# Tanh layer of a four-layer graph network on one Trainium2 core: the gate multiplies the vector weights first, the products go unreduced into the one-hot matmul in four column quadrants, and are folded once per group

## The reference, cut to what matters

```python
xs = concatenate([x[src, :8], x[dst, :8]])                 # 16 scalars per edge
xv = concatenate([x[src, 8:].reshape(E, 8, 3), x[dst, 8:].reshape(E, 8, 3)])
y1, y2 = _sph(edge_vec)
h = 2.0 ** 0.5 * relu(emb @ W1 / 10.0 ** 0.5)              # 16 hidden numbers per edge
w = (h @ W2 / 16.0 ** 0.5).reshape(E, 7, 16, 8)
wa_s, wb_s, wa_g, wb_g, wc, wd, we = [w[:, i] for i in range(7)]
s_out = PW_S * (einsum('eu,euw->ew', xs, wa_s) + INV_SQRT3 * einsum('eui,ei,euw->ew', xv, y1, wb_s))
g_out = PW_S * (einsum('eu,euw->ew', xs, wa_g) + INV_SQRT3 * einsum('eui,ei,euw->ew', xv, y1, wb_g))
v_out = PW_V * (INV_SQRT3 * einsum('eu,ek,euw->ewk', xs, y1, wc) + INV_SQRT3 * einsum('eui,euw->ewi', xv, wd)
                + einsum('eui,ea,iak,euw->ewk', xv, y2, W3J121, we))
s_act, gates = TANH_GAIN * tanh(s_out), TANH_GAIN * tanh(g_out)
edge_ftr = concatenate([s_act, (gates[:, :, None] * v_out).reshape(E, 24)]) * norm[:, None]
return segment_sum(edge_ftr, edge_dst, num_segments=N)
```

## Time and profile before

| | us |
|---|---|
| median of 3 runs (15111.97 to 15116.88) | 15116.87 |
| span of the profiled execution | 15106.0 |
| what lies around the span, against the median | 10.87 |
| stage of `window_pass_1` (first to last `prod`) | 4497.2 to 9752.3 |
| busy over the whole span: VectorE / TensorE matmuls | 12521.1 / 11855.8 |

### The profile page before, as it was taken

How to read it: one execution, slowest core, us unless ns; L and a number is a source line. 1 busy time by engine, 2 the same in 40 slices (tenths; PEclk the granted TensorE clock), 3 DMA queues, 4 the chain that set the end, 5 groups by cost and what they waited for, 6 DMA issues and landing times. The chain is left out here.

```text
span 15106.0 us, 424021 instructions
## 1 busy us (share of the span) xinstructions
PE 11855.8 (78%) x109342; PEld 9054.1 (60%) x109342; DVE 12521.1 (83%) x29790; ACT 7431.3 (49%) x23180; POOL 9508.3 (63%) x10157
## 2 busy tenths in 40 slices
PE   1555555555559999999999999967788888888888
PEld 1444444444446666666666666744566666666666
DVE  5777777777759999999999999910499999999998
ACT  0555555555536666666666666500144444444443
POOL 4777777777756666666666666400377777777775
PEclk8666667666669999999999999989899999999999
DMA  3666666666642222222221112179411111111111
GB/s 93 122 127 126 127 127 127 127 126 127 126 80 37 36 36 36 36 36 36 36 36 36 36 36 36 27 300 408 155 24 24 24 24 24 24 24 24 24 24 23
DMA packets 2705870, 1153.64 MB, mean 76 GB/s; under 512 B 2232498, under 2 KB 2650073, under 8 KB 2704124
## 3 DMA queue, kind: packets, MB, share of 16 engines
q1 hardware_dynamic: 2212179, 930.36, 26.0%
q0 software_dynamic: 312320, 178.52, 8.4%
q10 hardware_dynamic: 181250, 43.25, 1.4%
HBM read 767.02 MB, written 383.38 MB: 76 GB/s over the span
## 5 line engine op out<-in xcount | busy, mean ns | idle before, releaser
L1350 POOL DMA_INDIRECT w_rows<-table,w_idx x9375 | 8915.7, 951 | 4084.7 <-issue 2359.8
L1581 PE MATMUL w_p_w<-w_w,w_ht 128*128 128x256 f32 x12500 | 3007.0, 388 | 130.9 <-DVE w_prodv L1525 130.4
L1333 PE MATMUL w_p_deg<-w_hot_lo,w_hot_row 128*128 128x196 bf16 x6250 | 1825.7, 339 | 1588.9 <-DVE w_hot_lo L1278 1550.6
L1581 PEld LDWEIGHTS w_p_w<-w_w,w_ht 128*128 128x128 f32 x12500 | 2273.8, 190 | 678.4 <-issue 305.3
L1146 ACT ACTIVATE w_dist<-row_iota,w_negrel 128x32 f32<-128x32 f32 x9375 | 2181.8, 314 | 307.5 <-issue 282.4
L1791 DVE TENSOR_TENSOR w_prod<-w_p_xe,w_he 128x512 f32<-128x512 f32 x3125 | 2132.9, 683 | 3.2 <-PE w_p_xe L1934 3.1
L1552 ACT ACTIVATE w_ht<-w_p_h 128x512 f32<-128x512 f32 x1875 | 851.3, 527 | 2479.8 <-PE w_p_h L1572 2479.8
L1307 ACT CAST w_counts<-w_p_count 128x784 bf16<-128x784 f32 x1875 | 1251.1, 706 | 1438.9 <-PE w_p_count L1334 1429.6
L1333 PEld LDWEIGHTS w_p_deg<-w_hot_lo,w_hot_row 128*128 128x128 bf16 x6250 | 839.4, 134 | 1719.5 <-issue 1627.0
L1334 PE MATMUL w_p_count<-w_hot_lo,w_hot_row 128*128 128x196 bf16 x6250 | 1839.2, 340 | 0.0
L1957 PE MATMUL w_p_sgt<-w_prod,w_wc 128*32 128x128 f32 x25000 | 1330.9, 284 | 85.5 <-ACT w_sgt L1870 70.4
(11 more groups left out here) (208 smaller groups left out, 18953.5 us busy)
## 6 DMA issues: line engine op xcount, KB each, us to landing
counts<-w_counts SPq DMA_DIRECT2D x1250, 245.0 KB
d_rows<-counts SPq DMA_DIRECT2D x388, 784.0 KB
w_rows<-table,w_idx POOLq DMA_INDIRECT x9375
w_rel_row<-rel_row SPq DMA_DIRECT2D x625, 120.0 KB
w_edge<-e SPq DMA_DIRECT2D x625, 80.0 KB
w_idx<-src SPq DMA_DIRECT2D x1875, 2.5 KB
w_negrel<-negrel SPq DMA_DIRECT2D x1875, 2.5 KB
w_nodes<-split SPq DMA_DIRECT2D x1875, 2.0 KB
```

The source lines that it names most:

```text
L1333: nc.tensor.matmul(p_deg[:], hot_row[s2][:, b, :], hot_lo[s2][:, b, :], start=False, stop=False, skip_group_check=True)
L1350: pool.indirect_dma_start(out=rows[:, t, :], out_offset=None, in_=table[0:N, :], in_offset=bass.IndirectOffsetOnAxis(ap=idx[:, t:t + 1], a ...
L1581: last = nc.tensor.matmul(p_w[(g.base * len(BANKS) + bank) % WBANKS][:, (t - t0) * 256:(t - t0 + 1) * 256], ht[g.slot(UNROLL)][:, k, t * P ...
```

## The change

The vector weights `p_wv` move from group at(3) to at(4) and are made in one piece, after the gate's Tanh. The gate then multiplies all 128 of them for each edge (`gated_weights`, one multiplication of 128 x 640 into `mix`). The products with the source's vectors are made from `mix` into `mix` (three of 128 x 320), the along part of 8 numbers is gated apart and multiplied by the unit vector, and nothing is reduced per edge. Each edge now has 8 x 36 numbers of message. `QuarterSums.sum_edges`, for group at(5), takes the one-hot as the weights (32 columns, so one column quadrant of the array per tile) and the 288 numbers as the moving side: tiles 0 to 3 go to the quadrants 0 to 3, and tile 4 is spread over them in four pieces of 72 columns. `fold` copies and reduces the sums of the window once per group, and `sum_quarters` adds the four quadrants and turns the result over with one matmul. `add_window` follows for group at(5). ScalarE no longer copies the destination half of `p_wv` and copies the along part instead. `p_out` moves from `p_low` to the second bank of `p_wv`. In the new order `sum_edges` is the first thing in TensorE's step, `fold` stands on VectorE behind tile 1, and `wg.product` waits by `free(pe, w.acc_added, g, 4)` for `add_window` of group at(5) of the same step. `window_sums` treats 72 rows where there were 64; the one-hot rows of a group are made a step later.

```diff
+class QuarterSums:
+    def sum_edges(self, pe, g, tile, rest):
+        hot, matmul = self.hot[g.slot(UNROLL)], self.nc.tensor.matmul
+        done(pe, self.hot_ready, g)
+        free(pe, self.acc_added, g, 1)
+        pe.nop(nofuse=True)
+        for q in range(4):
+            matmul(self.p_mix[WIN * q:WIN * (q + 1), :], hot[:, q, :], tile(q), start=True, stop=False, skip_group_check=True)
+        for q in range(4):
+            columns, part = rest(q)
+            last = matmul(self.p_mix[WIN * q:WIN * (q + 1), columns], hot[:, 4, :], part, start=False, stop=True, skip_group_check=True)
+        last.then_inc(self.mix_ready, 1)
+    def sum_quarters(self, pe, g):
+        done(pe, self.held_ready, g)
+        self.nc.tensor.matmul(self.p_acc, self.held[g.slot(2)][:], self.a["stack_d"][:], start=True, stop=True).then_inc(self.acc_ready, 1)
...
+            def gates(g):
+                s2 = g.slot(2)
+                done(dve, bent_ready, g)
+                free(dve, gate_copied, g, 2)
+                vec.scalar_tensor_tensor(gate[s2][:], bent[s2][:], TANH_GAIN, spread(weight[g.slot(UNROLL)][:], [P, T, 16], 2),
+                                         ALU.mult, ALU.mult).then_inc(gate_ready, 1)
+            def gated_weights(g):
+                s2 = g.slot(2)
+                done(dve, along_ready, g)
+                done(dve, gate_ready, g)
+                free(dve, msg_ready, g, 1)
+                vec.tensor_mul(gated[:], along[s2][:], gate[s2][:, :, 8:16]).then_inc(gated_ready, 1)
+                done(dve, wv_ready, g)
+                free(dve, w.mix_ready, g, 2)
+                vec.tensor_mul(mix[s2][:, :, :, 0:ENDS], p_ends, spread(gate[s2][:, :, 8:16], [P, T, 8, ENDS], 3)).then_inc(wv_used, 1)
             def vector_products(g):
+                s, to = g.slot(UNROLL), mix[g.slot(2)]
+                done(dve, wv_used, g)
                 for k in range(3):
+                    vec.tensor_mul(to[:, :, :, 17 + 9 * k:25 + 9 * k], to[:, :, :, 0:8], spread(v16[s][:, :, 0:8, k], [P, T, 8, 8], 2))
+                done(dve, gated_ready, g)
+                vec.tensor_mul(to[:, :, :, 17:SLOT].rearrange("p t w (k u) -> p t w k u", u=9)[:, :, :, :, 8], spread(gated[:], [P, T, 8, 3], 3),
+                               spread(unit[s][:], [P, T, 8, 3], 2)).then_inc(msg_ready, 1)
+            def fold(g):
+                held, p_mix = w.held[g.slot(2)], w.p_mix.rearrange("p (w c) -> p w c", c=OWN)
+                done(dve, w.mix_ready, g)
+                free(dve, w.acc_ready, g, 2)
+                vec.tensor_copy(held[:, 0:72].rearrange("p (w c) -> p w c", c=9), p_mix[:, :, 0:9])
+                vec.tensor_reduce(held[:, 72:MSG1].rearrange("p (w k) -> p w k", k=3), p_mix[:, :, 9:OWN].rearrange("p w (k u) -> p w k u", u=9),
+                                  AX.X, ALU.add).then_inc(w.held_ready, 1)
...
+            def vector_weights(g):
+                done(pe, bent_ready, g)
+                done(pe, along_ready, g)
+                free(pe, wv_used, g, 1)
+                for t in range(T):
                     last = nc.tensor.matmul(p_wv[:, t * P:(t + 1) * P], he[g.slot(UNROLL)][:, t * P:(t + 1) * P], wv[:], start=True, stop=True)
+                last.then_inc(wv_ready, 1)
...
                 if g := at(1):
                     s = g.slot(UNROLL)
                     arrived(pe, loaded_a, g, LOADS_A)
-                    free(pe, gate_ready, g, 3)
-                    free(pe, vout_ready, g, 3)
+                    free(pe, w.acc_added, g, 4)
                     free(pe, dst_copied, g, 1)
                     wg.product(pe, g)
...
+                if g := at(4):
+                    vector_weights(g)
```

More of the change, by code:

```diff
@@ L1167, in add_window, with __init__, one_hot @@
         self.nc.vector.tensor_add(nodes, nodes, self.p_accs[g.slot(self.accs)]).then_inc(self.acc_added, 1)
+class QuarterSums:
+    def __init__(self, nc, a, layer, sb, p_mix, p_acc, width):
+        self.nc, self.a, self.width, sem = nc, a, width, a["sems"][layer]
+        self.p_mix, self.p_acc = p_mix, p_acc
+        self.dist = [sb(f"dist{s}", [P, T, WIN]) for s in range(2)]
+        self.hot = [sb(f"hot{s}", [P, T, WIN]) for s in range(UNROLL)]
+        self.held = [sb(f"held{s}", [P, width]) for s in range(2)]
+        self.dist_ready, self.hot_ready, self.mix_ready, self.held_ready, self.acc_ready, self.acc_added = (
+            sem(n) for n in ("dist_ready", "hot_ready", "mix_ready", "held_ready", "acc_ready", "acc_added"))
+    def one_hot(self, act, g, negrel):
+        dist = self.dist[g.slot(2)]
+        free(act, self.hot_ready, g, 2)
+        for t in range(T):
+            last = self.nc.scalar.activation(dist[:, t, :], self.a["row_iota"][:, 0:WIN], ACT.Abs, bias=negrel[:, t:t + 1])
+        last.then_inc(self.dist_ready, 1)
+        done(act, self.dist_ready, g)
+        free(act, self.mix_ready, g, UNROLL)
+        self.nc.scalar.activation(self.hot[g.slot(UNROLL)][:], dist[:], ACT.Relu, scale=-1.0, bias=1.0).then_inc(self.hot_ready, 1)
+    def sum_edges(self, pe, g, tile, rest):
[12 more added lines that the diff above has]
+        self.nc.tensor.matmul(self.p_acc, self.held[g.slot(2)][:], self.a["stack_d"][:], start=True, stop=True).then_inc(self.acc_ready, 1)
+    def add_window(self, dve, g):
+        base = dve.value_load(self.a["base_sb"][0:1, bass.ds(g.times(1), 1)], min_val=0, max_val=N - 1)
+        done(dve, self.acc_ready, g)
+        free(dve, self.acc_added, g, 1)
+        nodes = self.a["acc_t"][0:self.width, bass.ds(base, WIN)]
+        self.nc.vector.tensor_add(nodes, nodes, self.p_acc).then_inc(self.acc_added, 1)
@@ L1813, in step @@
                     tile_products(g, 1)
+                if g := at(5):
+                    fold(g)
                 if g := at(2):
@@ L1964, in step @@
             def step(at):
+                if g := at(5):
+                    done(pe, msg_ready, g)
+                    done(pe, gate_copied, g)
+                    pe.wait_ge(dst_copied, g.times(1, 4) if at(2) else G)
+                    w.sum_edges(pe, g, lambda t: tile(g, t), lambda q: quarter(g, q))
                 if g := at(3):
@@ L2013, in step @@
                     last.then_inc(xt_mm, 1)
-                if g := at(4):
-                    done(pe, gate_copied, g)
-                    pe.wait_ge(dst_copied, g.times(1, 4) if at(1) else G)
-                    w.sum_window(pe, g, msg[g.slot(2)], msg_ready)
             pipeline(pe, step)
```

122 lines of the change are left out of this document (44 added, 78 removed).

## The result

| | before | after |
|---|---|---|
| median, us | 15115.23 (4 runs, 15111.97 to 15116.88) | 18934.33 (4 runs, 18920.88 to 18970.41) |
| ratio, 95% interval | | 1.2532 [1.2514, 1.255] |
| span of the profiled execution, us | 15106.0 | 18968.7 |

The kernel is 25.3% slower. The forecast was 8.7% slower (16430 us), and 17000 us was the upper end of the range: the direction was right, the size was not.

The account below looks back on a forecast made before the run. Neither VectorE nor TensorE alone was taken to bound the loop, but their handovers within a step. (10.5 - 8.41) x 625 = 1306 us, plus 5, on 15106.0 plus 10.87 gave 16428, rounded to 16430 us; range 16100 to 17000.

Parts of the forecast that it names:

- The chain: Loop step from one `sum_edges` to the next, through TensorE and VectorE handovers: 10.5 us against 8.41 before.
- the main cause named: TensorE's queue: vector weights stand behind `wg.product`, which waits for `add_window`; VectorE then idles 2.06 us for them.
- a step without that wait: Rival: the wait of `wg.product` costs little, vector weights come 1.16 us earlier; step 9.4 us, 15750 us; chance 0.07.
- VectorE's terms: VectorE per group: 3.58 us removed, 2.91 added, so 0.67 less to do, between 0.3 and 0.9.
- the along part by the unit vector: VectorE multiplication writing 120 numbers, priced by size at 0.22 us.
- The clock: TensorE's matmuls on the chain priced at full-clock lengths; the vector weights' ten records take 1.38 us to their result.
- the clock falls: Rival: TensorE idles about 3 of 10.5 us; step 11.5 at clock 0.85, near 13 at 0.68; chance 0.17.
- The quadrants: TensorE's `sum_edges` streams four quadrants side by side in 0.75 us; rival, they don't: 2.7, kernel 17680 us, chance 0.04.
- VectorE's load decides: Rival, not slower: the step follows VectorE's load, 7.74 us, 14700 us in all; chance 0.04.
- the milder half of the clock's rival: TensorE's mean clock near 0.85: step 11.5 us, 17060 us; for it the range was taken as 16100 to 17000.

Follow-up runs that it names:

- e9_filled_less: Kernel after with the along part by the unit vector ahead of tile 3 and unread matmuls in TensorE's pauses, 5 ahead of `sum_edges`: 16560.53 us, ratio 1.0958.
- e6_weights_first: Kernel after with the along part by the unit vector ahead of tile 3 and the vector weights ahead of `wg.product` on TensorE: 15588.53 us, ratio 1.0315.
- e1: Kernel after with the along part by the unit vector (L1868) made right behind the gated weights, ahead of tile 3: 16928.83 us, ratio 1.12.
- e8: Kernel after with GpSimd's dots behind its first gather of the step instead of ahead of it: 17799.11 us, ratio 1.1777.
- e2: Kernel after with matmuls whose results nothing reads filling three TensorE pauses, 13 of them ahead of `sum_edges`: 17188.62 us, ratio 1.1372.
- e5: Kernel after with the edits of e1 and e2 together, 13 fill matmuls ahead of `sum_edges`: 17123.51 us, ratio 1.133.
- e12: Kernel after with each engine's work reordered, vector products a step later, GpSimd's dots waiting for the finished message: 15031.78 us, ratio 0.9944 to the kernel before.

## Why the prediction was right in direction and wrong in size

- **The chain** (right). 10.5 us was forecast for it, and `e9_filled_less` has 10.72 with the clock held and the dots elsewhere. The starts in the step shown agree to 0.2 us up to the vector weights. `e6_weights_first` shows the main cause named, the vector weights behind the wait of `wg.product`: 2.15 us against e1, 1.55 against e9. Its 9.17 is near the 9.4 that the prediction had for a step without that wait.
- **VectorE's terms.** The gated weights took 0.74 by the distance to the next instruction (0.80 forecast), a product 0.51 by its record less 0.08 (0.45), the fold 0.14 and 0.29 as forecast. The term that failed is the along part by the unit vector: 0.22 forecast by size, 1.16 measured to the next instruction (1.26 by its record). Without the dots beside it the next instruction starts 0.20 after it (e8, 8012.44 to 8012.64; 0.36 by its record), so its own size was right and 0.9 to 1.0 is contention with the dots. The forecast named who is queued behind whom on each engine, but never asked what runs beside VectorE's new instructions on GpSimd. With the clock held the two versions differ by 11.73 - 10.72 = 1.0 us per step, 630 us of the pass. The two differ in their fill too; with equal fill (e2, e5) the difference is only 0.1, since in e5 the fill stood in the way of the earlier message.
- **The clock** (the step that failed). The sum took every matmul on the chain at its length at the full clock, the vector weights for one at 1.38 where they took 2.45. The rival "the clock falls" had a chance of 0.17, on the ground that the earlier trace rows bracket the busy share and that the old loop's short waits went with a clock of 1.00. The trace of before had waits of 0.23 to 0.37 us in it, and the new order pauses of 1.3 and 2.0. The row did not bear on that. The rival's own price, near 13 us at 0.68, was near: 14.56 at 0.70 is that and the contention. The loss by the clock is 14.56 - 11.73 = 2.8 us per step, some 1770 us, the larger part of what was missed.
- **They multiply.** The contention lengthens the pause ahead of `sum_edges`, the pause lowers the clock, and the matmuls behind it, at the low clock, lengthen the wait ahead of the next part. So 0.90 us taken from L1868 gave 3.24 (e1). As a sum: 10.5 forecast, 0.2 for what `e9_filled_less` has above it, 1.0 for the contention, 2.8 for the clock, 14.5 of 14.56. The split between the last two depends on the order in which they are taken away.
- **The quadrants** (right). The first eight records of `sum_edges` and the next eight are through in 0.75 us at the full clock.
- **VectorE's load decides** (not so, in this order). It took a rewritten order (e12) to come below the time before.
- The range was too narrow because it took in only the milder half of the clock's rival and gave the contention nothing.

The prediction cited the Trainium skill's page TensorE: Matmul & The Clock Gate, the part on a second failure mode of the clock gate, for idle times between groups of matmuls that make the clock swing, and set it aside for the trace of before. The trace of after agrees with the page: the clock swings between 1.00 and 0.50, with 0.50 behind the two pauses of the step shown.

## What to carry to other kernels

Before you price a new order by the lengths of its instructions, list the pauses that it gives TensorE and compare them with pauses at which this program's clock is known to hold; if the new ones are longer and long matmuls stand behind them on the chain, price the chain at the low clock too. For each new VectorE instruction that reads only SBUF ask what GpSimd does at that moment, and give GpSimd's own work a wait that puts it beside instructions that read PSUM. When a matmul that needs little is queued behind one that waits for another engine, change places first: here that was worth 2.15 of 11.32 us (1.55 with the clock held), more than the 0.42 us of VectorE's time that the change saved.
